# Masked graph attention on one core: the order of two VectorE instructions behind a turn of tokens

## What is computed

```python
h = jnp.maximum(_layernorm(x, axis=-1), 0.0)
q = _split_heads(h @ Wq + bq)
k = _split_heads(h @ Wk + bk)
v = _split_heads(h @ Wv + bv)
scores = jnp.einsum('bhqd,bhkd->bhqk', q, k) / jnp.sqrt(jnp.asarray(HD, h.dtype))
scores = scores + beta * adj_e
scores = jnp.where(adj_e > 0, scores, jnp.asarray(-9000000000000000.0, scores.dtype))
probs = jax.nn.softmax(scores, axis=-1)
out = jnp.einsum('bhqk,bhkd->bhqd', probs, v)
x = x + out.transpose(0, 2, 1, 3).reshape(...)
```

## Time and profile before

| | |
|---|---|
| median of 3 runs | 1078.22 us (1078.0 to 1079.44) |
| the profiled execution | 1079.27 us |
| its span, first to last instruction | 1077.4 us |
| busy in it: TensorE, VectorE, ScalarE, GpSimd | 1020.8, 967.6, 884.5, 567.5 us |
| mean granted clock of TensorE | 0.992 |

### The profile page before, as it was taken

The page is one execution under the profiler, slowest core; times in us unless marked ns, Lnnn a source line. Parts: engine busy times, 40 slices in busy tenths (PEclk is TensorE's granted clock), DMA queues, the critical chain, the costliest instruction groups (busy, mean ns, idle before and its releaser), DMA issues. The chain is left out here.

```text
span 1077.4 us, 33776 instructions
## 1 busy us (share of the span) xinstructions
PE 1020.8 (95%) x10959; PEld 709.7 (66%) x10959; DVE 967.6 (90%) x4343; ACT 884.5 (82%) x2343; POOL 567.5 (53%) x756
## 2 busy tenths in 40 slices
PE   3899999999999999999999999999999999999986
PEld 2466676666666666666666667666666666667664
DVE  6579998999899999999999999999999999999897
ACT  3378888888888888888888888888888888888887
POOL 3645655445665445565444565544565544565431
PEclk9899999999999999999999999999999999999997
DMA  5454445554444554444554444554444554444441
GB/s 156 108 132 129 113 127 139 158 134 127 107 133 132 157 138 129 111 129 136 150 140 132 111 130 129 150 145 134 130 107 132 144 150 134 130 104 135 117 116 41
DMA packets 91038, 138.79 MB, mean 129 GB/s; under 512 B 15600, under 2 KB 66288, under 8 KB 90864
## 3 DMA queue, kind: packets, MB, share of 16 engines
q1 hardware_dynamic: 90336, 135.85, 47.1%
q10 hardware_dynamic: 528, 0.79, 0.2%
HBM read 35.91 MB, written 25.17 MB: 57 GB/s over the span
## 5 line engine op out<-in xcount | busy, mean ns | idle before, releaser
L523 ACT ACTIVATE probs<-biased,neg_max 128x128 f32<-128x128 f32 x1536 | 490.5, 390 | 146.9 <-DVE neg_max L638 115.5
L437 PE MATMUL ps_p<-hT,w 128*128 128x512 f16 x1728 | 423.5, 382 | 23.9 <-DVE hT L609 18.7
L638 DVE CUSTOM_DVE_ANT_0 biased<-ps_s,mask 128x128 f32<-128x128 f32 x1536 | 353.5, 286 | 75.8 <-PE ps_s L458 74.5
L336 POOL TENSOR_TENSOR on<-on,xb 128x384 f32<-128x384 f32 x128 | 128.0, 1000 | 380.9 <-DVE on L659 380.1
L437 PEld LDWEIGHTS ps_p<-hT,w 128*128 128x128 f16 x1728 | 167.5, 98 | 175.7 <-DVE hT L609 26.1
L644 DVE TENSOR_TENSOR pT<-ps_t,pT 128x512 f16<-128x512 f32 x384 | 263.3, 686 | 0.9 <-ACT pT L548 0.9
L466 PE MATMUL ps_t<-ident,probs 128*128 128x128 f32 x1536 | 245.4, 283 | 0.1
L548 ACT ACTIVATE pT<-ps_t 128x512 f16<-128x512 f32 x384 | 220.5, 574 | 1.0 <-PE ps_t L466 1.0
L437 PE MATMUL ps_p<-w,hT 128*128 128x384 f16 x1152 | 207.6, 326 | 0.0
L458 PEld LDWEIGHTS ps_s<-k_st,q_st 96*128 96x128 f16 x1536 | 117.5, 97 | 81.3 <-DVE neg_max L638 6.9
L481 PE MATMUL ps_o<-v,pT 128*128 128x33 f16 x1536 | 157.1, 179 | 8.9 <-DVE pT L644 5.2
(11 more groups left out here) (62 smaller groups left out, 1016.8 us busy)
## 6 DMA issues: line engine op xcount, KB each, us to landing
q_st<-qT SPq DMA_DIRECT2D x384, 96.0 KB, 2.2
k_st<-kT SPq DMA_DIRECT2D x384, 96.0 KB, 2.2
out<-on SPq DMA_DIRECT2D x128, 192.0 KB, 2.1
xs<-in_x SPq DMA_DIRECT2D x31, 768.0 KB, 5.0
adjs<-in_adj SPq DMA_DIRECT2D x32, 256.0 KB, 5.0
xs<-in_x ACTq DMA_DIRECT2D x1, 768.0 KB, 7.1
k_st<-in_L_gnn_Wq SPq DMA_DIRECT2D x1, 576.0 KB, 5.6
k_st<-in_L_gnn_Wk SPq DMA_DIRECT2D x1, 576.0 KB, 9.3
```

The lines of the kernel that those rows point to most:

```text
L336: pool.tensor_tensor(on[:, j % 2, :], on[:, j % 2, :], xb[:, par, j, :], ALU.add).then_inc(added, 1)
L437: mm = pe.matmul(dst, stationary, moving, start=m == 0, stop=m == MMS - 1)
L523: act.activation(probs[:, odd, i, :], biased[:, odd, i, :], ACT.Exp, bias=neg_max[:, odd, i:i + 1], scale=-1.0).then_inc(exp_done, 1)
L638: dve.tensor_tensor_reduce(out=biased[:, odd, i, :], in0=ps_s[:, i * N:(i + 1) * N], in1=mask[:, gp, v // CH, :], scale=-1.0, scalar=3.0e3 ...
```

## The change

In a slot behind one in which ("turn", 0) ended, VectorE issues `low_parts` ahead of `p_low`; in all other slots the order stays `p_low`, then `low_parts`. This is slot 6 of a step.

```diff
@@ -667,9 +667,13 @@
                     ended = valued is not None and valued[3] % CH == CH - 1
                     if scored:
                         bias_scores(*scored, (u - LAG) % 2)
+
+                    turn_first = u >= 1 and proj and any(UNITS[o] == ("turn", 0) for o in ENDED[u - 1])
+                    if turn_first:
+                        low_parts(s, par, u - 1, ahead)
                     if turned_late:
                         p_low(turned_late[0], (u - LAG) % 2)
-                    if u >= 1 and proj:
+                    if u >= 1 and proj and not turn_first:
                         low_parts(s, par, u - 1, ahead)
                     if u == 0 and s >= 1:
                         low_parts(s - 1, 1 - par, SLOTS - 1, s <= STEPS - 1)
```

## The result

| | before | after |
|---|---|---|
| median | 1078.72 us (1078.0 to 1079.44, 4 runs) | 1061.24 us (1060.15 to 1062.6, 4 runs) |
| profiled execution, span | 1079.27, 1077.4 us | 1062.6, 1060.7 us |

The ratio is 0.9839, 95% interval 0.9822 to 0.9856: 17.5 us or 1.6% less, where 18.0 us less had been forecast.

What follows compares the result with a forecast made beforehand. The prediction took TensorE's wait for VectorE's L609 in slot 6, held up by pT, as the bound: 30 steps x 0.60 us = 18.0 us off the median 1078.22 gives 1060.2 us, range 1057.0 to 1067.0.

Steps and rivals of the forecast that it cites:

- What bounds it: Slot 6: TensorE's first matmul of ("k", 2) waits for VectorE's L609, 18.7 us in 30 times; full stall 0.80 us.
- the 0.60 us of pT: Slot 6, VectorE: pT (L644) runs before L609 and delays the first matmul of ("k", 2), which needs nothing of it.
- The turn's low part first: Slot 6: L609 starts at 515.64 instead of 516.24 without a new wait, so ("k", 2) starts 0.60 us earlier.
- 0.74 us to the matmul: Slot 6: time from the start of L609 to the first matmul of ("k", 2), taken as unchanged.
- 0.20 us of stall left: Slot 6: ("k", 2) would start at 516.38, still 0.20 us behind the 516.18 at which TensorE is ready.
- The probabilities' low part second: Slot 6: pT starts 0.60 us later, covered by VectorE's 1.06 us idle time; slot 7's values (L481) lose nothing.
- The 0.81 us: From pT's new start to slot 7's values, against 0.74 to 0.83 seen elsewhere; possible loss 0.02 us a step.
- 30 new waits of L481: Sign in the changed profile: slot 7's values waiting for pT would show the claim of no loss there wrong.
- What reaches the end of the step: From slot 7 on: all 0.60 us passes through; ScalarE's exponentials move only 0.38 us but still end before they are needed.
- the rival of the half gain: Slot 7: ScalarE's 0.38 us limits what reaches slot 8; gain 11.4 us, time 1066.8; chance 0.09.
- the one of VectorE's total: Whole step: VectorE, busy 29.67 of 32.08 us, is the bound; nothing gained, 1078.2 us; chance 0.05.
- the next standing item of the steps: In TensorE's list of waits, the item after the 18.7 us wait for L609: 5.2 us in 17 times.

Runs made afterwards that it cites:

- ps_between: Changed kernel plus, in 30 steps, a VectorE 128 x 128 subtraction with one PSUM operand between slot 6's two low parts; 1061.8 us, ratio 0.9833.
- pad_between: Changed kernel plus, in 30 steps, a spare VectorE 128 x 128 addition of SBUF operands between slot 6's two low parts; 1075.5 us, ratio 0.9956.
- scalar_spare: Changed kernel plus a spare 128 x 128 copy on ScalarE behind its work of slot 6; 1061.37 us, ratio 0.983.
- ps_ahead: Changed kernel plus, in 30 steps, a VectorE 128 x 128 subtraction with one PSUM operand ahead of both low parts of slot 6; 1067.73 us, ratio 0.989.
- mask_slot9: Changed kernel with the linking of the mask (L603) in slot 9 instead of slot 7; 1051.19 us, ratio 0.9735.
- pad_behind3: Changed kernel plus, in 30 steps, three spare VectorE 128 x 128 additions of SBUF operands behind both low parts of slot 6; 1065.95 us, ratio 0.987.

## Why the prediction was right

*What bounds it.* The time measured is 1.0 us above the 1060.2 forecast: 0.5 us because the median before came to 1078.72 with a fourth run, 0.5 us because the gain was 17.5 and not 18.0, of which 0.2 us lie in the steps. That the 0.60 us of pT lay on the path is shown twice over: by their going, and by spare instructions of 0.39 and 0.21 us at the same place, which came back at 0.39 and 0.20 us a step. (The rows of the chain that the forecast places "a few steps later" are 15 steps later; nothing else rests on that.)

*The turn's low part first.* No new wait for its high part, 0.74 us to the matmul, 0.20 us of stall left: all as worked out.

*The probabilities' low part second.* The 0.81 us were there to the hundredth and cost nothing. But the text called this "the narrowest cover of the change" and set its price, if gone, at the missing part of the 0.81 us. That was wrong: ps_between took 0.20 us of it, TensorE waited 0.13 us, and the time did not move. The wait of slot 9 for pT is set by VectorE, whose slots 7 and 8 run without a gap from the scores of slot 7; TensorE may lose up to 0.41 us between slot 7's values and slot 10 and only waits less later on. Only what is beyond that is paid, as in pad_between. The scores of slot 7 are the point that counts, and they stand ahead of the values. Nor would the sign that the forecast named for this part, 30 new waits of L481, have shown a short wait: the 0.13 us of ps_between are booked nowhere.

*What reaches the end of the step.* 0.593 of 0.60 us a step; the rival of the half gain fell with scalar_spare, the one of VectorE's total with the pair ps_ahead and ps_between. The forecast had set a rule beside that last rival. The Trainium skill, "Perfetto Trace Analysis", section "Identifying the Most-Contended Engine", says that the engine with the highest occupancy is to be optimised first. By the busy shares here that is VectorE with its 90%, and the swap takes no work from it: VectorE is as busy as before and the kernel is 1.6% faster. The gaps, and what ended them, told more than the shares.

*A reading that was off.* The 5.2 us in 17 times of TensorE's wait for pT were called the next standing item of the steps. The item reads 4.9 us in 16 times after the change, and the standing waits of slots 9 and 10 are not in it: 0.29 and 0.12 us fit under the modelled ends of the matmuls and are booked as busy. mask_slot9 shows that they were real, 0.41 us a step. They are found by comparing starts, not by reading the list of waits.

## What to carry to other kernels

When two instructions of a busy engine have different waiters, the one whose waiter stands still goes first; before it is moved, compare for the other the distance from its start to its reader with the shortest such distance in the trace. The same swap in slots 7 and 9 as well was worth minus 0.60 us a step, so a rule for all places is no substitute for asking at each who waits. And a wait costs only if no later wait, set by another engine, takes it back.

## What the runs showed of the hardware

A VectorE addition of two SBUF operands, 128 x 128 in float32, took 0.28 us at the shortest and up to 1.01 us beside a GpSimd addition. In pad_between 28 of the 30 began while GpSimd's L322 was running, and each ended 0.15 us behind it; of the two that took 0.28 us, one had no GpSimd instruction beside it and one began 0.15 us before L322 did. In pad_behind3 the first of three additions in a row ran beside L322 and took 0.41 us in the median, the two behind it 0.28 us each. The profile of pad_between has the spread over its 30 instructions (duration in ns, min, median, max):

```profile
L666 DVE TENSOR_TENSOR spare<-ident x30: 280/1005/1012, 66.3 to 993.3; 128x128 f32<-128x128 f32 x30
```

With one operand in PSUM at the same place:

```profile
L666 DVE TENSOR_TENSOR spare<-ps_t,ident x30: 280/280/282, 66.2 to 981.2; 128x128 f32<-128x128 f32 x30
```

The Trainium skill, "SBUF — State Buffer", section "SBUF: two separate sides", states it: VectorE and GpSimd share a pair of ports as an exclusive lock, which a VectorE instruction with two SBUF inputs takes against a GpSimd instruction that reads SBUF, and the loser is held for the whole instruction. This case's trace agrees for VectorE as the one that is held, 1.005 us against 0.280; no run here shows a GpSimd instruction held. The kernel's own VectorE instructions of slot 6 each have an operand in PSUM, so the swap did not meet it; a spare instruction for an experiment has to be of the kind of its neighbours.
